# Router scores with the router weights stationary, an earlier load of the projection weights, and an expert-weight row copied from PSUM, in a transformer layer with eight experts

## The chip, the cores and the metric

The kernel runs on all 8 cores of one Trainium2 chip, each core doing one of the 8 batch elements with the same program. The metric is the device time of the slowest core in microseconds; lower is better.

## The reference

x is 8 x 2048 x 1024. The layer is attention, a residual and a layer norm, then a mixture of experts, a residual and a layer norm:

```python
x = _layernorm(x + _L0_attn_ref(x, W_attn, b_attn, W_proj, b_proj))
x = _layernorm(x + _L0_ffn_ref(x, router_w, ..., down_b))
...
scores = h @ router_w.T + router_b
vals, idx = jax.lax.top_k(scores, TOP_K)
vals = jax.nn.softmax(vals, axis=-1)
cw = jnp.sum(jax.nn.one_hot(idx, N_EXPERTS) * vals[..., None], axis=1)
for e in range(N_EXPERTS):
    g = h @ gate_up_w[e].T + gate_up_b[e]
    out = out + (_swiglu(g) @ down_w[e].T + down_b[e]) * cw[:, e:e + 1]
```

There are 16 heads of 64, rotary embedding, causal attention, 8 experts of hidden size 1024, and the two best experts of each token have weight. The kernel computes all 8 experts for all tokens; cw is zero for the others.

## The kernel before

Activations lie with features on the 128 partitions: 8 chunks of 128 features, 2048 tokens along the free axis, handled in 4 stretches (tt) of 512 tokens. A core goes through five stages one after the other.

1. QKV (L455, L476), bf16 matmuls with float32 sums in PSUM.
2. Attention, two heads at a time: scores (L647, L653), exponential on ScalarE (L664), mask on GpSimd (L672), sum with V (L686, L693). VectorE takes each result out of PSUM (ytst, L711) and SyncE stores it to ys_d in DRAM.
3. Projection and first layer norm, by tt. SyncE loads the softmax sums (srow) and then the attention result (ytsl) from ys_d, ScalarE's or SyncE's queue the residual (xfsl). The inverse sums are spread by a matmul with the selection matrix sel (pbc, L858), VectorE scales ytsl (L863), then 64 matmuls with wproj (pp, L878), residual, bias, and the layer norm in float32 in acc (`_ln_stats`, `_ln_apply`). `_ln_apply` spreads two rows of 512 float32 values with one-row matmuls (L252, L254). The result goes as bf16 to x1_d.
4. Router, in float32 from acc: scores (prt, L979), copied from PSUM to sctm (L987), top two and softmax on VectorE and ScalarE (L991 to L1029) into cwtm, 16 transposes (L1041), and a copy to cwT16 (L1045), which holds one expert's weights in each of 8 rows. cwrow0 is a zeroed tile of 128 partitions whose row 0 holds the current expert's row; a matmul with ones (pcw, L1228) spreads it.
5. Experts: for each e and tt, 8 times 8 gate matmuls (pg, L1283) and 8 up matmuls (pu, L1291), the activation, and the down matmuls of the stretch before (pd, L1136). Expert weights (wg in two halves, lo and hi; wd) are loaded ahead by SyncE and GpSimd. The last layer norm ends the program.

Each engine runs its instructions in the order in which they are written, and each DMA is issued from an engine's queue: channels dy0 to dy4 are SyncE's, dg0 to dg2 GpSimd's, dsc0 and dsc1 ScalarE's. Every channel has a semaphore. `E.dma` (L81) waits until the DMA issued last on its channel has landed. `E.w(consumer, tokens)` puts a wait into one engine's queue. `E.bar()` gives the present count of every engine's and every channel's semaphore, so `E.w("dy", *E.bar())` stops SyncE until all that has been issued so far in the program's text is done, DMAs included:

```python
    def bar(self):
        return tuple((k, self.cnt[k]) for k in self.cnt)
```

Such a wait for everything stands ahead of stage 3 on the queues of GpSimd, SyncE and ScalarE (dg, dy, dsc), because the tiles of that stage lie where attention's lay, and again ahead of stage 5.

Of the kernel before, what the change touches and what calls it, by code (L numbers as in the profile page):

```python
# [7 lines left out]
F32 = mybir.dt.float32  # L8
BF16 = mybir.dt.bfloat16
# [4 lines left out]
T = 2048  # L14
D = 1024
NCH = 8
NEXP = 8
# [258 lines left out]
def build_nc():  # L276
    nc = bass.Bass("TRN2", target_bir_lowering=False)
# [41 lines left out]
    with ExitStack() as st:  # L319
        a = st.enter_context  # L320
        E = Emit(nc, st)
        pe, act, dve = nc.tensor, nc.scalar, nc.vector
# [3 lines left out]
        rwt = a(nc.sbuf_tensor("rwt_s", [128, NCH * NEXP], F32))  # L326
# [11 lines left out]
        cwT16 = a(nc.sbuf_tensor("cwT16", [128, T], BF16))  # L338

        t_bqk = E.dma("dy4", bqk[:], bqk_i)  # L340
        t_bproj = E.dma("dy3", bproj[:], bproj_i)
        t_rwt = E.dma("dy2", rwt[:], rwt_i)
        t_rbr = E.dma("dy1", rbr_row[:], rbr_i)
        tok_zpad = E.tk(dve.memset(dbt16[:], 0.0), "dve")
        tok_zcw = E.tk(dve.memset(cwT16[:], 0.0), "dve")
        E.w("dg", tok_zpad)
# [8 lines left out]
        with nc.sbuf_tensor("gub_s", [128, NEXP * 16], F32) as gub, \  # L355
# [4 lines left out]
            for e2 in range(NEXP):  # L360
# [13 lines left out]
            tok_mm = E.tk(pe.matmul(pbi[:, 0:8], onesrf[0:1, :], rbr_row[0:1, :],  # L374
                                    start=True, stop=True), "pe")
# [4 lines left out]
        t_attn_done = None  # L380
        t_yt_dma = None
        with ExitStack() as s12:
# [25 lines left out]
            with ExitStack() as s1:  # L408
# [23 lines left out]
                with nc.psum_tensor("pq0", [128, 512], F32) as pq0, \  # L432
# [8 lines left out]
                    for tt in range(4):  # L441
                        par = tt % 2
# [298 lines left out]
        with ExitStack() as s3:  # L741
# [13 lines left out]
                    for i in range(2)]  # L755
# [11 lines left out]
            E.w("dg", *E.bar())  # L767
            E.w("dy", *E.bar())
            E.w("dsc", *E.bar())
            t_sel = E.dma("dg0", sel16[:], sel_i)  # L770
            rs_z = [E.tk(dve.memset(rs16[i][:], 0.0), "dve") for i in range(2)]
# [3 lines left out]
                           wproj_i[:, p * QWP:(p + 1) * QWP]) for p in range(4)]  # L775

# [193 lines left out]

            with nc.psum_tensor("prt2", [128, 128], F32) as prt2:
                E.mode(("mm", "k128", "f32"))
                mm_last = None
                for tt in range(4):
                    E.w("pe", t_rwt, tok_ln1_mul[tt])
                    for q_ in range(4):
                        ti = tt * 4 + q_
                        for c in range(NCH):
                            mm_last = pe.matmul(  # L979
                                prt2[:, ti * NEXP:(ti + 1) * NEXP],  # L980
                                acc[:, c * T + tt * 512 + q_ * 128:
                                    c * T + tt * 512 + (q_ + 1) * 128],
                                rwt[:, c * NEXP:(c + 1) * NEXP],
                                start=(c == 0), stop=(c == NCH - 1))
                tok_mm = E.tk(mm_last, "pe")
                E.w("dve", tok_mm)
                tok_sctm = E.tk(dve.tensor_copy(sctm[:], prt2[:, 0:128]), "dve")  # L987
                E.w("pe", tok_sctm)
# [47 lines left out]
            with nc.psum_tensor("prt3", [128, 2048], F32) as prt3:  # L1036
                E.mode(("tr", "f32"))
                E.w("pe", tok_cw, t_id)
                tr_tok = None
                for ti in range(16):  # L1040
                    tr = pe.transpose(prt3[0:NEXP, ti * 128:(ti + 1) * 128],  # L1041
                                      cwtm[:, ti * 8:(ti + 1) * 8], ident[:, 0:128])
                    tr_tok = E.tk(tr, "pe")
                E.w("dve", tr_tok)
                tok_cwT16 = E.tk(dve.tensor_copy(cwT16[0:NEXP, :],  # L1045
                                                 prt3[0:NEXP, 0:2048]), "dve")
                E.w("pe", tok_cwT16)

        dbias_ev = {}
        with ExitStack() as s5:  # L1050
# [9 lines left out]
            cwrow0 = b5(nc.sbuf_tensor("cwrow0", [128, T], BF16))  # L1060
# [33 lines left out]
            tok_crz = E.tk(dve.memset(cwrow0[:], 0.0), "dve")  # L1094
            E.w("dg", tok_cwT16, tok_crz)
            t_cwrow = [E.dma("dg0", cwrow[0][0:1, :], cwT16[0:1, :]), None]
# [307 lines left out]
```

How the kernel before makes its waits and increments, by code:

```python
    def tk(self, instr, key, step=1):  # L45
        self.cnt[key] += step
        instr.then_inc(self.sem[key], step)
        return (key, self.cnt[key])
# [1 line left out]
    def w(self, consumer, *tokens):  # L50
        eng = self.eng[consumer]
        best = {}
        for tok in tokens:
            if tok is None:
                continue
            key, val = tok
            if val > best.get(key, -1):
                best[key] = val
        for key, val in best.items():
            ck = (consumer, key)
            if self.wcache.get(ck, 0) >= val:
                continue
            eng.wait_ge(self.sem[key], val)
            self.wcache[ck] = val
# [9 lines left out]
    def dma(self, ch, out, in_):  # L74
        eng = self.dmaeng[ch]
        if self.cnt[ch]:
            ck = ("q" + ch, ch)
            if self.wcache.get(ck, 0) < self.cnt[ch]:
                eng.wait_ge(self.sem[ch], self.cnt[ch])
                self.wcache[ck] = self.cnt[ch]
        return self.tk(eng.dma_start(out=out, in_=in_), ch, 16)
```

## Time and profile before

| | |
|---|---|
| median of the runs shown | 2650.16 us (two runs: 2594.32 and 2706.0) |
| the profiled execution's own time | 2439.51 us |
| its span, slowest of the cores (core 3) | 2437.9 us |
| span of the fastest core (core 0) | 2424.8 us |
| mean granted TensorE clock, core 3 | 0.907 |

### The profile page before, as it was taken

The numbers are of one execution on the slowest core, as the hardware profiler recorded it, in microseconds if no ns is written. First come the engines' busy times: TensorE is split into PE (matmuls) and PEld (weight loads), VectorE is DVE, ScalarE is ACT, GpSimd is POOL, SyncE is SP. The second block draws the span as 40 slices with busy tenths as digits, with TensorE's granted clock in tenths as the row PEclk, the third lists the DMA queues.
The fourth block names the chain that finished last, engine by engine and source line by source line (L and its number), as shares of the span: only waits on it lengthen the run. The fifth ranks groups of instructions, "written<-read, shape, count | busy, mean of one in ns | idle before, by whom it ended". The sixth has DMA issues, their size and how long they took to land.

```text
span 2437.9 us, 26649 instructions; the slowest of 8 cores (2424.8 to 2437.9 us)
## 1 busy us (share of the span) xinstructions
PE 2062.6 (85%) x8982; PEld 912.7 (37%) x8982; DVE 933.4 (38%) x1982; ACT 942.0 (39%) x1336; POOL 162.0 (7%) x248
## 2 busy tenths in 40 slices
PE   6996776777745766999999999999999999999974
PEld 2442222222212254443443443443444444444431
DVE  3106323232025431444444444444444443444456
ACT  2233666666624520432332332332333333333541
POOL 1000222111110100000000000000000000000100
PEclk9997888888867855999999999999999999999986
DMA  6300111111054023110301301301302113011002
GB/s 147 52 13 14 33 28 27 27 27 27 10 145 121 18 70 121 69 35 20 128 26 35 121 18 35 122 18 35 121 18 92 64 35 121 18 35 52 18 31 108
DMA packets 39978, 137.67 MB, mean 56 GB/s; under 512 B 5852, under 2 KB 19549, under 8 KB 30886
## 3 DMA queue, kind: packets, MB, share of 16 engines
q1 hardware_dynamic: 27412, 83.95, 10.7%
q0 software_dynamic: 9888, 47.30, 6.2%
q10 hardware_dynamic: 2546, 4.72, 0.6%
q8 instruction: 75, 1.23, 0.2%
q14 instruction: 57, 0.47, 0.1%
HBM read 116.28 MB, written 16.84 MB: 55 GB/s over the span
## 4 chain that ended last, share of the span: by engine, by line
PE 74%; ACT 8%; DVE 7%; DMA 4%; issue 4%; POOL 2%; DVEq 0%; ACTq 0%; SPq 0%; POOLq 0%
PE pg L1283 18%; PE pu L1291 18%; PE pd L1136 18%; ACT attAB L664 6%; PE pq L455 3%; PE pp L878 3%; PE psy L686 3%; PE pv L476 2%; PE prt L979 2%; POOL attAB L672 2%; DVE acc L264 2%; DVE acc L261 2%; PE psab L653 2%; PE psy L693 2%; PE psab L647 2%
## 5 line engine op out<-in xcount | busy, mean ns | idle before, releaser
L1304 ACT ACTIVATE sgt<-pg,gubs_s 128x512 bf16<-128x512 f32 x256 | 176.3, 689 | 920.0 <-PE pu L1291 887.3
L1283 PE MATMUL pg<-x1sl,wg 128*128 128x512 bf16 x2048 | 492.3, 384 | 4.1 <-DMA wg<-wg 4.1
L1136 PE MATMUL pd<-as,wd 128*128 128x512 bf16 x2048 | 484.9, 380 | 12.7 <-DVE acc L1146 12.1
L1291 PE MATMUL pu<-x1sl,wg 128*128 128x512 bf16 x2048 | 484.8, 380 | 0.0
L664 ACT ACTIVATE attAB<-psab,consts_s 128x1024 bf16<-128x1024 f32 (+1 forms) x320 | 302.7, 985 | 189.1 <-PE psab L653 188.2
L1319 DVE TENSOR_SCALAR gct<-gct 128x512 bf16<-128x512 bf16 x256 | 75.2, 294 | 748.6 <-ACT uct L1312 748.6
L1283 PEld LDWEIGHTS pg<-x1sl,wg 128*128 128x128 bf16 x2048 | 202.3, 99 | 252.7 <-issue 17.4
L1136 PEld LDWEIGHTS pd<-as,wd 128*128 128x128 bf16 x2048 | 200.6, 98 | 257.0 <-issue 17.3
L1291 PEld LDWEIGHTS pu<-x1sl,wg 128*128 128x128 bf16 x2048 | 200.8, 98 | 243.0 <-issue 2.4
L686 PE MATMUL psy<-attAB,vaug 128*65 128x512 bf16 (+1 forms) x320 | 124.2, 388 | 142.4 <-POOL attAB L672 88.2
L1146 DVE TENSOR_TENSOR acc<-acc,pd 128x512 f32<-128x512 f32 x256 | 174.1, 680 | 8.8 <-PE pd L1136 8.8
L1312 ACT ACTIVATE uct<-pu,gub_s 128x512 bf16<-128x512 f32 x256 | 176.9, 691 | 0.0
L1308 ACT ACTIVATE gct<-pg,gub_s 128x512 bf16<-128x512 f32 x256 | 174.6, 682 | 0.0
L711 DVE CAST ytst<-psy 65x1024 bf16<-65x1024 f32 x32 | 38.9, 1218 | 259.0 <-PE psy L693 209.6
L686 PEld LDWEIGHTS psy<-attAB,vaug 128*65 128x65 bf16 x320 | 37.4, 117 | 268.6 <-issue 267.7
L647 PE MATMUL psab<-qkraw 128*128 128x512 bf16 (+1 forms) x320 | 127.9, 400 | 7.6 <-DVE qkraw L597 7.6
L653 PE MATMUL psab<-qkraw,kpadB 128*128 128x512 bf16 (+1 forms) x320 | 126.9, 397 | 0.0
L693 PE MATMUL psy<-attAB,vaug 128*65 128x512 bf16 (+1 forms) x320 | 125.1, 391 | 0.0
L672 POOL TENSOR_TENSOR attAB<-attAB,cmask_s 128x256 bf16<-128x256 bf16 x128 | 93.5, 739 | 467.8 <-ACT attAB L664 465.5
L455 PE MATMUL pq<-xsl,wqk 128*128 128x512 bf16 x512 | 112.6, 382 | 11.2 <-DMA wqk<-wqk 11.2
L1337 DVE TENSOR_TENSOR as<-gct,uct 128x512 bf16<-128x512 bf16 x256 | 108.8, 425 | 28.4 <-DVE uct L1329 2.3
L1326 DVE TENSOR_TENSOR gct<-gct,sgt 128x512 bf16<-128x512 bf16 x256 | 107.5, 420 | 1.5 <-DVE uct L1322 1.5
(154 smaller groups left out, 1344.1 us busy)
## 6 DMA issues: line engine op xcount, KB each, us to landing
x1sl<-x_d SPq DMA_DIRECT2D x30, 1024.0 KB
wg<-wg SPq DMA_DIRECT2D x8, 2048.0 KB
wg<-wg POOLq DMA_DIRECT2D x8, 2048.0 KB, 17.0
wd<-wd POOLq DMA_DIRECT2D x14, 1024.0 KB, 5.5
out<-acc SPq DMA_DIRECT2D x29, 256.0 KB, 2.3
qswp<-qkraw SPq DMA_DIRECT2D x56, 128.0 KB
ys_d<-ytst SPq DMA_DIRECT2D x64, 65.0 KB
xsl<-x_t POOLq DMA_DIRECT2D x4, 1024.0 KB, 11.2
```

The lines of the kernel that those rows point to most:

```text
L455: mm_last = pe.matmul(pq[mp][:, 0:512], wqk16[:, (m * NCH + c) * 128:(m * NCH + c + 1) * 128], xsl[par][:, c * 512:(c + 1) * 512], start=( ...
L647: mA = pe.matmul(psAB[par][:, 0:w_], qkraw[:, kcol + 128 * j:kcol + 128 * j + 128], qkraw[:, qcol + tqs:qcol + tq0 + 512], start=True, sto ...
L653: mB = pe.matmul(psAB[par][:, 512:512 + w_], kpadB[:, cch * T + 128 * j:cch * T + 128 * j + 128], qkraw[:, qcol + tqs:qcol + tq0 + 512], s ...
L664: eAB = act.activation(dst3, src3, AF.Exp, bias=consts[:, 0:1], scale=0.125)
L686: aA = pe.matmul(psy[qp][0:65, tqs - tq0:512], vaug[:, j * 1056 + hA * 66: j * 1056 + hA * 66 + 65], attAB[ab][:, 0:w_], start=(j == 0), s ...
L1136: mmd = pe.matmul(pd[dp][:, 0:512], wdb[:, (m2_ * NCH + hc_) * 128:(m2_ * NCH + hc_ + 1) * 128], asb[tp_][:, hc_ * 512:(hc_ + 1) * 512], s ...
L1146: tok = E.tk(dve.tensor_tensor(acc[:, sl], acc[:, sl], pd[dp][:, 0:512], ALU.add), "dve")
L1283: mmg = pe.matmul(pg[hp][:, 0:512], wgb[ep][:, (hc * NCH + c) * 128:(hc * NCH + c + 1) * 128], x1sl[k % 2][:, c * 512:(c + 1) * 512], star ...
L1291: mmu = pe.matmul(pu[hp][:, 0:512], wgb[ep][:, ((hc + 8) * NCH + c) * 128: ((hc + 8) * NCH + c + 1) * 128], x1sl[k % 2][:, c * 512:(c + 1) ...
L1304: tok_sg = E.tk(act.activation(sg_t[hp][:], pg[hp][:], AF.Sigmoid, bias=gubs[:, bg:bg + 1], scale=1.702), "act")
L1308: tok_rg = E.tk(act.activation(gc_t[hp][:], pg[hp][:], AF.Relu, bias=gub7[:, bg:bg + 1], scale=1.0), "act")
L1312: tok_ru = E.tk(act.activation(uc_t[hp][:], pu[hp][:], AF.Relu, bias=gub7[:, bu:bu + 1], scale=1.0), "act")
```

## The change

There are three edits.

The router's scores are computed the other way round. Before, a slice of acc of 128 features by 128 tokens was stationary and the 8 columns of router weights moved past it (128 matmuls of the program). Now the 128 x 8 router weights are stationary and 512 tokens of acc move (32 matmuls). The result lies as 8 rows by 512 tokens, so VectorE copies it to sct after each stretch, and 16 transposes bring it into the shape that the following code expects.

```diff
+            with nc.psum_tensor("prt0", [128, 512], F32) as prt0, \
+                 nc.psum_tensor("prt1", [128, 512], F32) as prt1:
+                E.mode(("mm", "k128m8", "f32"))
+                sc_ev = []
+                for tt in range(4):
+                    par = tt % 2
+                    if tt >= 2:
+                        E.w("pe", sc_ev[tt - 2])
+                    E.w("pe", t_rwt, tok_ln1_mul[tt])
+                    mm_last = None
+                    for c in range(NCH):
+                        mm_last = pe.matmul(
+                            [prt0, prt1][par][0:NEXP, 0:512],
+                            rwt[:, c * NEXP:(c + 1) * NEXP],
+                            acc[:, c * T + tt * 512:c * T + (tt + 1) * 512],
+                            start=(c == 0), stop=(c == NCH - 1))
+                    tok_mm = E.tk(mm_last, "pe")
+                    E.w("dve", tok_mm)
+                    iv = dve.tensor_copy(sct[:, tt * 512:(tt + 1) * 512],
+                                         [prt0, prt1][par][0:NEXP, 0:512])
+                    sc_ev.append(E.tk(iv, "dve"))
...
-                        for c in range(NCH):
-                            mm_last = pe.matmul(
-                                prt2[:, ti * NEXP:(ti + 1) * NEXP],
-                                acc[:, c * T + tt * 512 + q_ * 128:
-                                    c * T + tt * 512 + (q_ + 1) * 128],
-                                rwt[:, c * NEXP:(c + 1) * NEXP],
-                                start=(c == 0), stop=(c == NCH - 1))
...
+                E.w("pe", t_id, *sc_ev)
+                for ti in range(16):
+                    tr = pe.transpose(prt2[:, ti * 8:(ti + 1) * 8],
+                                      sct[:, ti * 128:(ti + 1) * 128],
+                                      ident[0:8, 0:8])
```

On TensorE this is, from the end of the last layer norm to the transposes of the gate weights (prt is the scores' PSUM tile, acc the activations, rwt_s the router weights, sct the scores by rows, cwtm the gate weights), before:

```order
L252 MATMUL plb<-srB,onesrf_s 128x512 [waits sem_act,sem_dve]
L254 MATMUL plb<-srC,onesrf_s 128x512
L979 MATMUL prt<-rwt_s,acc 128x8 [waits sem_act]
L979 MATMUL prt<-rwt_s,acc 128x8 x95
L979 MATMUL prt<-rwt_s,acc 128x8 [waits sem_dve]
L979 MATMUL prt<-rwt_s,acc 128x8 x31
L1041 MATMUL prt<-ident_s,cwtm 8x128 [waits sem_dve,sem_dy4]
L1041 MATMUL prt<-ident_s,cwtm 8x128 x15
```

and now:

```order
L254 MATMUL plb<-srC,onesrf_s 128x512
L986 MATMUL prt<-acc,rwt_s 8x512 [waits sem_act]
L986 MATMUL prt<-acc,rwt_s 8x512 x15
L986 MATMUL prt<-acc,rwt_s 8x512 [waits sem_dve]
L986 MATMUL prt<-acc,rwt_s 8x512 x7
L986 MATMUL prt<-acc,rwt_s 8x512 [waits sem_dve]
L986 MATMUL prt<-acc,rwt_s 8x512 x7
L1003 MATMUL prt<-ident_s,sct 128x8 [waits sem_dve,sem_dy4]
L1003 MATMUL prt<-ident_s,sct 128x8 x15
L1062 MATMUL prt<-ident_s,cwtm 8x128 [waits sem_dve]
```

The 128 matmuls have become 32 and 16 transposes, and both runs of matmuls start on the same wait, for ScalarE's last cast of the layer norm.

Ahead of stage 3 the loads of sel and of the four quarters of wproj are issued before the wait for everything, when the last attention result is out of PSUM (t_attn_done). The wait itself now stands behind them:

```diff
-            E.w("dg", *E.bar())
-            E.w("dy", *E.bar())
-            E.w("dsc", *E.bar())
+            E.w("dg", t_attn_done)
+            E.w("dy", t_attn_done)
             t_sel = E.dma("dg0", sel16[:], sel_i)
-            rs_z = [E.tk(dve.memset(rs16[i][:], 0.0), "dve") for i in range(2)]
             QWP = 2 * NCH * 128
             t_wp4 = [E.dma(("dg0", "dg1", "dg2", "dy4")[p],
                            wproj16[:, p * QWP:(p + 1) * QWP],
                            wproj_i[:, p * QWP:(p + 1) * QWP]) for p in range(4)]
+            E.w("dg", *E.bar())
+            E.w("dy", *E.bar())
+            E.w("dsc", *E.bar())
+            rs_z = [E.tk(dve.memset(rs16[i][:], 0.0), "dve") for i in range(2)]
```

On SyncE's queue, from the last stores of attention to the first loads of the projection stage (- is before, + is now):

```order
 L81 DMA ys_d<-ytst 65x512 [waits sem_dve,sem_dy3]
 L81 DMA ys_d<-ytst 65x512 [waits sem_dy3]
-L81 DMA wproj<-wproj 128x2048 [waits sem_pe,sem_act,sem_pool,sem_dy0,sem_dy1,sem_dy2,sem_dy3,sem_dy4,sem_dg0,sem_dg1,sem_dg2,sem_dsc0,sem_dsc1]
-L81 DMA srow_0<-ys_d 8x512 [waits sem_dy0] x2
+L81 DMA wproj<-wproj 128x2048 [waits sem_dy4]
+L81 DMA srow_0<-ys_d 8x512 [waits sem_pe,sem_act,sem_pool,sem_dy0,sem_dy1,sem_dy2,sem_dy3,sem_dy4,sem_dg0,sem_dg1,sem_dg2,sem_dsc0,sem_dsc1]
+L81 DMA srow_0<-ys_d 8x512 [waits sem_dy0]
 L81 DMA ytsl<-ys_d 64x4096 [waits sem_dy0]
 L81 DMA ytsl<-ys_d 64x4096 [waits sem_dy1]
```

The long wait has moved from ahead of wproj to ahead of srow, and its counts of dg0, dg1, dg2 and dy4 now include the loads just issued.

Ahead of stage 5, row 0 of cwrow0 for the first expert is copied by VectorE straight from PSUM. cwrow0 is allocated and zeroed at the program's start; before, it was zeroed here and filled by a DMA on GpSimd's queue:

```diff
+                tok_cwr0 = E.tk(dve.tensor_copy(cwrow0[0:1, :],
+                                                prt3[0:1, 0:2048]), "dve")
...
-            tok_crz = E.tk(dve.memset(cwrow0[:], 0.0), "dve")
-            E.w("dg", tok_cwT16, tok_crz)
-            t_cwrow = [E.dma("dg0", cwrow[0][0:1, :], cwT16[0:1, :]), None]
+            E.w("dg", tok_cwT16)
+            t_cwrow = [tok_cwr0, None]
```

## Rows read from the trace of the kernel before

**Rows 1.** The page, part 2: granted TensorE clock in 40 slices, tenths

```profile
PEclk9997888888867855999999999999999999999986
```

**Rows 2.** The page, part 4: shares of the chain of waits, by line

```profile
PE pg L1283 18%; PE pu L1291 18%; PE pd L1136 18%; ACT attAB L664 6%; PE pq L455 3%; PE pp L878 3%; PE psy L686 3%; PE pv L476 2%; PE prt L979 2%; POOL attAB L672 2%; DVE acc L264 2%; DVE acc L261 2%; PE psab L653 2%; PE psy L693 2%; PE psab L647 2%
```

**Rows 3.** Groups of instructions: the router's matmuls and its weight loads; stationary size precedes moving

```profile
L979 PE MATMUL prt<-rwt_s,acc 128*128 128x8 f32 x256 | 54.8, 361 | 12.3 <-ACT x1b L270 12.3
L979 PEld LDWEIGHTS prt<-rwt_s,acc 128*128 128x128 f32 x256 | 54.7, 333 | 13.9 <-issue 13.9
```

**Rows 4.** Windows: us, busy (count) by engine, TensorE clock share, DMA share, GB/s

```profile
714.00:719.00 5.00, 4.85 (x12) 1.80 (x13) 0.69 (x2) 0.26 (x1) 0.00 (x0) 0.50 0.95 207
...
884.60:939.50 54.90, 54.78 (x256) 54.69 (x256) 0.00 (x0) 0.00 (x0) 0.00 (x0) 0.50 0.17 59
945.00:949.00 4.00, 3.22 (x16) 1.83 (x16) 0.42 (x2) 0.00 (x0) 0.00 (x0) 0.62 0.00 0
```

**Rows 5.** Chain of waits, float32 512-column matmuls: start us, us, what

```profile
851.63 0.87 PE plb L254 x2
...
870.62 1.72 PE plb L254 x2
```

**Rows 6.** Groups of instructions: float32 weight load of eight columns

```profile
L1041 PEld LDWEIGHTS prt<-ident_s,cwtm 128*8 128x8 f32 x16 | 1.8, 118 | 7.0 <-issue 5.9
```

**Rows 7.** Timeline, end of the layer norm and router: start us, us, engine, line

```profile
863.72 0.67 DVE L221 TENSOR_SCALAR srC<-pstat 1x512 f32<-1x512 f32 x1
...
884.66 54.78 PE L979 MATMUL prt<-rwt_s,acc 128*128 128x8 f32 x256 [12.34 <-ACT x1b L270]
...
939.55 0.29 DVE L987 COPY sctm<-prt 128x128 f32<-128x128 f32 x1 [55.92 <-PE prt L979]
```

**Rows 8.** Timeline, from gate weights to the load of wg

```profile
945.28 3.22 PE L1041 MATMUL prt<-ident_s,cwtm 128*8 128x128 f32 x16 [5.83 <-DVE cwtm L1029]
948.61 2.28 DVE L1045 CAST cwT<-prt 8x2048 bf16<-8x2048 f32 x1 [3.58 <-PE prt L1041]
951.26 1.76 DVE L1094 MEMSET cwrow<- 128x2048 bf16 x1 [0.38 <-issue]
951.57 0.33 SPq L81 DMA_DIRECT2D wg<-wg  x1
953.67 0.51 POOL L81 DMA_DIRECT2D cwrow<-cwT  x1 [101.07 <-DVE cwrow L1094]
954.18 0.55 POOL L81 DMA_DIRECT2D wg<-wg  x1
```

**Rows 9.** Timeline, first matmuls of the experts

```profile
967.80 3.57 PE L1283 MATMUL pg<-x1sl,wg 128*128 128x512 bf16 x8 [4.10 <-DMA wg<-wg]
```

**Rows 10.** Timeline, attention's end to the projection's start

```profile
677.96 1.99 SPq L81 DMA_DIRECT2D ys_d<-ytst  x2
681.68 0.36 SPq L81 DMA_DIRECT2D wproj<-wproj  x1
...
682.23 0.62 POOL L81 DMA_DIRECT2D sel<-sel  x1 [6.41 <-DMA ys_d<-ytst]
```

**Rows 11.** Chain of waits, same place

```profile
682.15 8.05 DMA srow<-ys_d
...
690.26 5.11 DMA srow<-ys_d
...
696.02 12.03 DMA ytsl<-ys_d
```

**Rows 12.** DMA issues: KB each, median us from issue to landing

```profile
wd<-wd POOLq DMA_DIRECT2D x14, 1024.0 KB, 5.5
...
wproj<-wproj POOLq DMA_DIRECT2D x3, 512.0 KB, 7.8
...
cc<-cc POOLq DMA_DIRECT2D x1, 512.0 KB, 5.8
...
sel<-sel POOLq DMA_DIRECT2D x1, 256.0 KB, 10.1
```

More of the change, by code:

```diff
@@ L338, in build_nc @@
         cwT16 = a(nc.sbuf_tensor("cwT16", [128, T], BF16))
+        cwrow0 = a(nc.sbuf_tensor("cwrow0", [128, T], BF16))
         t_bqk = E.dma("dy4", bqk[:], bqk_i)
@@ L345, in build_nc @@
         tok_zcw = E.tk(dve.memset(cwT16[:], 0.0), "dve")
+        tok_crz = E.tk(dve.memset(cwrow0[:], 0.0), "dve")
         E.w("dg", tok_zpad)
@@ L969, in r3 @@
                 return ap.rearrange("p (t e) -> p t e", e=NEXP)
-            with nc.psum_tensor("prt2", [128, 128], F32) as prt2:
[L972 to L977, printed above, removed]
-                        for c in range(NCH):
-                            mm_last = pe.matmul(
-                                prt2[:, ti * NEXP:(ti + 1) * NEXP],
-                                acc[:, c * T + tt * 512 + q_ * 128:
-                                    c * T + tt * 512 + (q_ + 1) * 128],
-                                rwt[:, c * NEXP:(c + 1) * NEXP],
-                                start=(c == 0), stop=(c == NCH - 1))
-                tok_mm = E.tk(mm_last, "pe")
-                E.w("dve", tok_mm)
+            with nc.psum_tensor("prt0", [128, 512], F32) as prt0, \
[19 more added lines that the diff above has]
+                    sc_ev.append(E.tk(iv, "dve"))
+                E.w("pe", *sc_ev)
@@ L987, in build_nc @@
+            with nc.psum_tensor("prt2", [128, 128], F32) as prt2:
+                E.mode(("tr", "f32"))
+                E.w("pe", t_id, *sc_ev)
+                tr_tok = None
+                for ti in range(16):
+                    tr = pe.transpose(prt2[:, ti * 8:(ti + 1) * 8],
+                                      sct[:, ti * 128:(ti + 1) * 128],
+                                      ident[0:8, 0:8])
+                    tr_tok = E.tk(tr, "pe")
+                E.w("dve", tr_tok)
                 tok_sctm = E.tk(dve.tensor_copy(sctm[:], prt2[:, 0:128]), "dve")
@@ L1037, in build_nc @@
                 E.mode(("tr", "f32"))
-                E.w("pe", tok_cw, t_id)
+                E.w("pe", tok_cw)
                 tr_tok = None
@@ L1043, in build_nc @@
                     tr_tok = E.tk(tr, "pe")
-                E.w("dve", tr_tok)
+                E.w("dve", tr_tok, tok_crz)
                 tok_cwT16 = E.tk(dve.tensor_copy(cwT16[0:NEXP, :],
                                                  prt3[0:NEXP, 0:2048]), "dve")
+                tok_cwr0 = E.tk(dve.tensor_copy(cwrow0[0:1, :],
+                                                prt3[0:1, 0:2048]), "dve")
                 E.w("pe", tok_cwT16)
@@ L1059, in build_nc @@
             cwb = b5(nc.sbuf_tensor("cwb16", [128, T], BF16))
-            cwrow0 = b5(nc.sbuf_tensor("cwrow0", [128, T], BF16))
             cwrow = [cwrow0, cwrow0]
```

## The prediction

> **What bounds the kernel now.** I read the spans of the cores first, then the chain of waits by line, then the clock row, then the stages that the change touches in windows and as a timeline. The chain says where a saved microsecond counts: gate, up and down matmuls hold 18% each, and the router's L979 holds 2% [rows 2], so nothing here can touch the bulk. But the router is a stretch where TensorE alone decides: its two records for each of 128 matmuls are busy 54.8 us, its weight loads 54.7 us [rows 3], nothing else runs, and VectorE waits 55.92 us for the end [rows 7]. The reader should see that the weight loads are as long as the matmuls: 54.78 / 256 = 0.214 us a record, for 8 moving columns. The clock row has its two lowest slices there [rows 1], and the window shows 0.50, 1.2 GHz, through all 54.9 us although the engine never paused [rows 4]. The other touched place is the hand-over from attention to the projection, where the chain runs through DMAs: srow 8.05, srow 5.11, ytsl 12.03 us [rows 11].
>
> **The router matmuls.** They leave with 54.78 us. In their place stand 32 matmuls of 512 moving float32 columns, two records each, so 64. The nearest rows are the one-row float32 matmuls of the layer norm, also 512 columns in two records: 0.87 us for the pair at high clock, 1.72 us at 1.2 GHz [rows 5]. So 64 records take 32 x 0.87 = 27.8 us, or 32 x 1.72 = 55.0 us at the low clock. Which one? The engine comes in at the low clock, after 12.34 us idle [rows 7]. After such an idle time the projection's bf16 matmuls of 512 columns ran at 0.50 for 5 us [rows 4] and the first 3.57 us of the experts were slow as well [rows 9]; then both went high. The L979 stream stayed low, but even the 16 transposes of 128 moving columns behind it, 3.22 us of work, sit in a window whose mean is 0.62 [rows 4, 8]. The two streams that rose were 512-column matmuls like the new ones, so I take their course, 3.5 to 5 us at half speed, which costs half of that, 2.2 us. The matmuls end 30.0 us after the same start, 884.66, at 914.7.
>
> Behind them is new work. VectorE's four PSUM copies of 8 x 512 overlap the matmuls but for the last: 0.67 us by a one-row op of that width [rows 7], and 0.2 us to start. Then TensorE restarts (0.25 us) and does 16 transposes. Their stationary side is 128 float32 columns, like the L979 loads at 0.214 us a record at the low clock; each transpose is one record (16 for 16 in rows 8), so 3.4 us at most and 1.7 us if the clock is high just behind the stream. I take 2.1 with the latency of the last, and 0.3 to the copy of sctm. Sum 884.66 + 30.0 + 0.2 + 0.67 + 0.25 + 2.1 + 0.3 = 918.2, against 939.55 [rows 7]: 21.3 us earlier. All that follows up to the experts hangs on this, one engine after the other, so it arrives whole. The identity matrix is loaded on SyncE's queue as before and is first needed some 30 us into the router rather than 60; nothing ahead of it is new.
>
> The eight-column weight loads are the open cost. One takes 118 ns [rows 6], and I count them at nothing because the load of the next record hides behind the 435 ns of the present one, as 128-column loads do inside the 0.87 us pair. The Trainium skill, "TensorE: Matmul & The Clock Gate", Part 3, says that a weight load overlaps a matmul in flight only when its row group differs, and here all use all 128 rows. By that rule 64 x 118 ns = 7.6 us would be added and the gain would be 13.7 us. The row of the pair speaks against it, though its weights have one row; I keep this as a rival.
>
> **The row for the first expert.** Before, from the start of the cwT16 copy at 948.61: copy 2.28, memset of cwrow to 953.02, cwrow's DMA at 953.67, wg lo at 954.18 on GpSimd; SyncE issues wg hi at 951.57 [rows 8]. Now the memset is at the program's start (1.76 us on VectorE, under the first loads) and a copy of 1 x 2048 follows. Its length is not in the trace; VectorE's time goes by the free size (0.67 us for one row of 512 above), so I take the 2.28 us of the 8-row copy. The count that both queues wait for now includes this copy: 948.61 + 2.28 + 0.1 + 2.28 = 953.27. GpSimd, 0.65 us later as before, issues wg lo at 953.9, 0.3 us earlier; SyncE, 0.68 us behind as before, issues wg hi at 953.95, 2.4 us later. The gate matmuls wait for lo (967.80, [rows 9]), and hi is wanted only one group of 8 matmuls later, 3.57 us. With hi's head start gone, lo gets no less of the DMA engines. I take -0.3 us, between -1 and +2. Queued behind on GpSimd is wd, not wanted before the second stretch.
>
> **The earlier load.** This is the part with two sides. The loads of sel and of the SyncE quarter of wproj go out some 4 and 1.7 us earlier, at about 678.1 and 680.0 instead of 682.23 and 681.68 [rows 10]. But the three waits for everything now stand behind them, and everything includes their own semaphores. SyncE may not issue srow, and ScalarE not xfsl, before all of wproj has landed. GpSimd still waits for sel before its first quarter (10.1 us, [rows 12]), with the other two behind it in the queue. Nobody else is queued there that matters: GpSimd's next work is a cast after the first projection matmuls.
> So, step by step: sel is half of cc, which took 5.8 us; alone I take 4.5, landing at 683.2. The three quarters, 1.5 MB, go out by 684.8 and land in 6.5 us or so (7.8 beside ytsl in rows 12, 1 MB of wd in 5.5): 691.5. SyncE then issues srow at 691.9 instead of 682.15, 9.8 us late. What comes back is contention: the first srow took 8.05 us beside sel, xfsl and a quarter of wproj; now only xfsl is beside it, as beside the second, 5.11 us. ytsl took 12.03 us beside 1.5 MB of wproj, now alone 5.6 us by the 1 MB wd row. Arrival: 691.9 + 5.1 + 5.1 + 0.9 + 5.6 = 708.6, against 696.02 + 12.03 = 708.05 [rows 11]. That is +0.5 us: the same bytes in another order, an earlier start against two more stops. From below: if the srow pair takes 2 x 2 us, -6. From above: sel 10.1 again, wproj 9, srow 8.05 and 5.11, ytsl 6, about +15.
>
> The srow step rests on order within a queue. By the Trainium skill, "DMA: Bandwidth & Descriptors", Queues, rings and completion order, each DMA engine takes turns between queue rows and works in order within one. Then the first srow stood behind SyncE's own quarter of wproj, and would not now, so it may fall below 5 us. Rows 11 only show that the first was slower than the second.
>
> **Sum.** -21.3 - 0.3 + 0.5 = -21.1 us of the profiled execution's 2439.5: 2418.4. The two timed runs have their median at 2650.2, 1.086 times the profiled time, and lie 4.3% apart. On that scale the same share of the time is 21.1 x 1.086 = 22.9 us, and 2650.2 - 22.9 gives 2627. I state this one, since it is to be held against runs like those shown, and the range must know both levels. The change is -0.9%; about 2% is what a measurement of this kernel can tell from no change.
>
> **Rivals.**
> 1. Slower: the clock stays at 1.2 GHz through the new router matmuls. For it: L979, back to back for 55 us, did not lift it [rows 4], and both streams are float32 with the same operands. Against: bf16 streams of that width rose, and the float32 pair kept 0.435 us a record behind one [rows 5]. Price: 55.0 + 0.2 + 0.67 + 0.25 + 3.4 + 0.3 = 59.8 us from 884.66, ending 944.5, 4.9 us late: 2444.6, or 2655.5 on the scale of the runs. It decides from a mean record of about 0.77 us, where the new stream with its tail equals the old. Chance 0.12.
> 2. The wait behind its own loads costs its upper bound, because sel needs 10 us even alone: +15, total -6: 2433.7 (2644). Chance 0.14. For it: GpSimd's casting load was the slowest of its size. Against: cc casts too, twice as large, in 5.8.
> 3. Weight loads are not hidden: -13.5, 2426.0 (2635.5). Chance 0.07.
> 4. The earlier load pays, -6 there: -27.6, 2411.9 (2620). Chance 0.09.
> 5. My forecast, a gain of 17 to 26 us: 0.58, its own range 2413 to 2423 on the profiled execution, 2622 to 2632 on the scale of the runs.
>
> All five lie within 2%, so 0.80 for no change that can be told. The rest is the scatter of runs 4.3% apart, leaning to the forecast's sign: faster 0.14, slower 0.06. The range is not set by the terms but by the level: it reaches from the profiled level with the full gain, 2411, to the higher run shown less the gain, 2706 - 23 = 2683.
>
> **What would show it.** Right: 64 router records of about 0.43 us with the clock at 1.0 after some 4 us; sctm's copy some 34 us after the last cast of the layer norm; wg hi issued beside lo; srow issued near 692 with all of wproj landed, and ytsl's first scaling near 708.6. Wrong: records near 0.85 us, weight loads standing between matmuls, the first pp matmul later than 716 or earlier than 710, or the experts' up matmuls waiting for wg hi.

## The result and the profile after

| | before | changed |
|---|---|---|
| median of all timed runs | 2463.5 us (10 runs, 2438.7 to 2759.0) | 2421.1 us (11 runs, 2418.3 to 2752.0) |
| ratio | | 0.9917, 95% interval 0.9904 to 0.9930 |
| profiled execution, its own time | 2439.5 us | 2418.7 us |
| span of the slowest core | 2437.9 us (core 3) | 2417.1 us (core 4) |
| mean granted clock of that core | 0.907 | 0.914 |

The change gains 0.83%, 20.2 us of 2440; the profiled executions are 20.8 us apart. Four of the eleven runs of the changed kernel (2510.8 to 2752.0 us) had the four cores of one die at 0.79 to 0.88 of full clock while the other die stayed near 0.915, and the ratio leaves such runs out.

The page of the changed kernel, the clock in 40 slices and the shares of the chain, which answer to [rows 1] and [rows 2]:

```profile
PEclk9997888888867777999999999999999999999986
...
PE pg L1304 19%; PE pu L1312 18%; PE pd L1157 18%; ACT attAB L666 6%; PE pq L457 5%; PE psy L688 3%; PE pp L882 3%; POOL attAB L674 2%; PE pv L478 2%; DVE acc L264 2%; PE psab L655 2%; PE psab L649 2%; DVE acc L261 2%; PE psy L695 2%; PE prt L986 1%
```

The two slices that were 5 are now 7, and the router's line has fallen from 2% to 1% of the chain. Gate, up and down stand as they did, within 1% of the span.

One core is not enough to place a microsecond: in the kernel before, the hand-over from attention takes 27.7 to 31.5 us on the eight cores. So the stages were read from the timelines of all eight, as the time between two starts, and the table gives the median over the cores.

| from start to start, us | before | changed | difference | forecast |
|---|---|---|---|---|
| last copy of attention's result (ytst) to first scaling of ytsl | 29.21 | 30.19 | +1.0 | +0.5 |
| to the first pp matmul | 6.01 | 6.01 | 0 | 0 |
| to the first router matmul | 169.53 | 169.60 | +0.1 | 0 |
| to the copy of sctm | 54.89 | 32.66 | -22.2 | -21.3 |
| to the copy of cwT16 | 9.12 | 9.30 | +0.2 | 0 |
| to the first expert matmul | 17.85 | 19.65 | +1.8 | -0.3 |
| to the end | 1469.70 | 1470.08 | +0.4 | 0 |

These add up to -18.7; the medians of stages need not add to the difference of two slowest cores.

The router first. Groups of instructions of the changed kernel, answering to [rows 3]:

```profile
L986 PE MATMUL prt<-acc,rwt_s 128*8 128x512 f32 x64 | 30.4, 640 | 12.3 <-ACT x1b L270 12.3
...
L986 PEld LDWEIGHTS prt<-acc,rwt_s 128*8 128x8 f32 x64 | 6.0, 94 | 37.4 <-issue 37.4
...
L1003 PE MATMUL prt<-ident_s,sct 8*128 8x8 f32 x16 | 1.1, 201 | 1.1 <-DVE sct L993 1.1
```

64 records stand in place of 256. The 64 weight loads are busy 6.0 us, but the matmuls take 30.4 us, against 27.8 us of streaming at the high clock and 2.2 us more for the slow start, so next to nothing of the 6.0 stands between them. The windows of the same stretch (us, then busy time and count of PE, PEld, DVE, ACT, POOL, then granted clock, DMA share, GB/s) show the slow start, which answers to [rows 4]:

```profile
883.70:888.00 4.30, 4.30 (x6) 0.72 (x7) 0.00 (x0) 0.00 (x0) 0.00 (x0) 0.50 0.71 244
888.00:890.00 2.00, 2.00 (x5) 0.38 (x4) 0.00 (x0) 0.00 (x0) 0.00 (x0) 0.67 0.00 0
890.00:900.00 10.00, 10.00 (x25) 2.07 (x23) 0.68 (x1) 0.00 (x0) 0.00 (x0) 1.00 0.64 217
900.00:913.00 13.00, 13.00 (x31) 2.70 (x30) 1.36 (x2) 0.00 (x0) 0.00 (x0) 1.00 0.01 1
```

For 4.3 us the clock is 0.50 and the window touches six records, in the next two it rises, and from 890 on the windows touch 25 in 10 us. The timeline of VectorE behind it, answering to [rows 7], has the last copy to sct and the copy of sctm:

```profile
914.20 0.68 DVE L993 COPY sct<-prt 8x512 f32<-8x512 f32 x1 [6.19 <-PE prt L986]
916.44 0.29 DVE L1008 COPY sctm<-prt 128x128 f32<-128x128 f32 x1 [1.55 <-PE prt L1003]
```

2.24 us lie between their starts. I had put 3.3; the 16 transposes take 1.1 us in all and not 2.1.

Then the start of the experts, answering to [rows 8] and [rows 9]:

```profile
925.75 2.28 DVE L1066 CAST cwT<-prt 8x2048 bf16<-8x2048 f32 x1 [3.82 <-PE prt L1062]
927.95 2.27 DVE L1068 CAST cwrow<-prt 1x2048 bf16<-1x2048 f32 x1
...
930.76 0.33 SPq L81 DMA_DIRECT2D wg<-wg  x1
931.33 0.53 POOL L81 DMA_DIRECT2D wg<-wg  x1 [79.54 <-issue]
...
946.97 3.57 PE L1304 MATMUL pg<-x1sl,wg 128*128 128x512 bf16 x8 [13.09 <-DMA wg<-wg]
```

The row copy takes 2.27 us, as forecast. Both halves of wg are now issued within 0.6 us of each other, and lo, 15.1 us after its issue has ended, is what the first gate matmul waits for; before, it was 13.1 us. The pcw matmuls, which spread the row and waited for cwrow's DMA before, are done long ahead and gain nothing.

The chain through the hand-over (start us, us, what), answering to [rows 11]:

```profile
679.04 4.01 DMA sel<-sel
...
684.67 7.81 DMA wproj<-wproj
...
692.69 2.82 DMA srow<-ys_d
...
695.59 4.70 DMA srow<-ys_d
...
700.94 6.76 DMA ytsl<-ys_d
```

sel takes 4.0 us instead of 10.1. All of wproj is down at 692.5, and only then may srow go; but srow is now 2.8 and 4.7 us instead of 8.1 and 5.1, ytsl 6.8 instead of 12.0. Over the eight cores the first srow took 4.7 to 8.0 us before and takes 1.4 to 3.1 now, ytsl 10.3 to 13.2 before and 6.5 to 7.8 now.

### The profile page after: what moved, and what is told of

The parts are those of the page before. It is cut to its first block, busy times and chain, and to the rows that moved or that the text cites. A ratio compares the mean times of both kernels' runs of the same rounds, so it can differ in the third digit from the quotient of the medians.

```text
span 2417.1 us, 26296 instructions; the slowest of 8 cores (2407.1 to 2417.1 us)
## 1 busy us (share of the span) xinstructions
PE 2042.8 (85%) x8806; PEld 866.4 (36%) x8806; DVE 938.2 (39%) x1987; ACT 939.6 (39%) x1336; POOL 160.8 (7%) x247
## 4 chain that ended last, share of the span: by engine, by line
PE 75%; ACT 8%; DVE 7%; issue 4%; DMA 3%; POOL 2%; DVEq 0%; ACTq 0%; POOLq 0%; SPq 0%
PE pg L1304 19%; PE pu L1312 18%; PE pd L1157 18%; ACT attAB L666 6%; PE pq L457 5%; PE psy L688 3%; PE pp L882 3%; POOL attAB L674 2%; PE pv L478 2%; DVE acc L264 2%; PE psab L655 2%; PE psab L649 2%; DVE acc L261 2%; PE psy L695 2%; PE prt L986 1%
## 5 line engine op out<-in xcount | busy, mean ns | idle before, releaser
L1304 PE MATMUL pg<-x1sl,wg 128*128 128x512 bf16 x2048 | 492.1, 384 | 13.1 <-DMA wg<-wg 13.1
L457 PE MATMUL pq<-xsl,wqk 128*128 128x512 bf16 x512 | 112.6, 382 | 10.2 <-DMA wqk<-wqk 9.3
```

The source lines that it names most:

```text
L457: mm_last = pe.matmul(pq[mp][:, 0:512], wqk16[:, (m * NCH + c) * 128:(m * NCH + c + 1) * 128], xsl[par][:, c * 512:(c + 1) * 512], start=( ...
L1304: mmg = pe.matmul(pg[hp][:, 0:512], wgb[ep][:, (hc * NCH + c) * 128:(hc * NCH + c + 1) * 128], x1sl[k % 2][:, c * 512:(c + 1) * 512], star ...
```

## The experiments

Eleven kernels were run. The first four take the change apart. Each ratio is to the kernel before, run on the same chip.

**router_only.** The kernel before with the router edit and nothing else.

> The kernel before with the router edit alone. Theory (each edit acts in its own stage and the stages are in series): the router, from its first matmul to the copy of sctm, shrinks from 54.9 to 32.8 us as in the changed kernel, the two other stages stay as before, and the time falls by 22 us (ratio 0.991). Rival (part of the gain comes from the other edits, or the experts' start takes some back because wg is then late): a gain of 18 us or less.

Measured: 2420.0 us, ratio 0.9920 (0.9902 to 0.9938). First router matmul to sctm 32.6 us, cwT16 to the first expert matmul 17.85 as before, hand-over 29.4. The theory holds: the router edit alone gives the whole gain. What the two other edits cost in the table, 2.8 us, is too little for the two kernels' times to show (2420.0 and 2421.1 us).

**load_only.** The kernel before with only the earlier load.

> The kernel before with the earlier load of sel and wproj alone. Theory (the same bytes in another order): from the last copy of the attention result to the first pp matmul 36.6 us instead of 37.5, so -0.9 us (ratio 0.9996). Rival (the difference of 0.9 us between the two profiles is scatter of the DMAs): anything between -3 and +3 us, and another split over sel, wproj, srow and ytsl than 4.0, 7.8, 2.8 + 4.7 and 6.8 us.

Measured: 2441.3 us, ratio 1.0002 (0.9991 to 1.0012). Over the hand-over its eight cores took 29.6 to 31.8 us, though in an execution of 2562.8 us. The other kernels settle it: in the four without the earlier load (before, router_only, cwrow_only, old_router_warmed) the eight-core medians are 29.0 to 29.4 us, in the six with it and with the wait behind it (the changed kernel, row_not_waited, wd_after_lo, router_128, router_in_the_gap, wg_early) 30.0 to 30.6. The gain of 0.9 us that I read from two slowest cores was the scatter of one core: the theory's sign is wrong, and the eight-core table, +1.0 us, is right. The split on core 3 is as in the changed kernel (sel 4.4, wproj 6.9, srow 3.0 and 4.6, ytsl 6.7).

**cwrow_only.** The kernel before with only the row copied from PSUM.

> The kernel before with the row for the first expert copied from PSUM alone. Theory (wg hi loses its head start of 2.6 us, all three weight loads start together and wg lo lands later): from the start of the cwT16 copy to the first expert matmul 21.2 us instead of 19.2, +2.0 us in all (ratio 1.0008). Rival (the 2 us belong to the earlier time at which the load falls in the changed kernel, or to scatter): 19.2 us as before, +-0.3 us.

Measured: 2443.2 us, ratio 1.0012 (1.0002 to 1.0023). cwT16 to the first expert matmul: median 20.2 us against 17.85, so +2.35. This edit takes away a DMA and a memset and still costs time, and its interval lies above 1.

**wait_old_counts.** The changed kernel, with the wait taken from older counts:

```diff
+            bar0 = E.bar()
             E.w("dg", t_attn_done)
             E.w("dy", t_attn_done)
...
-            E.w("dg", *E.bar())
-            E.w("dy", *E.bar())
-            E.w("dsc", *E.bar())
+            E.w("dg", *bar0)
+            E.w("dy", *bar0)
+            E.w("dsc", *bar0)
```

> The changed kernel, with the wait for everything ahead of the projection stage taken from counts read before the loads of sel and wproj are issued, so it waits for attention only. Theory (the same bytes with fewer stops): srow is issued near 682 again, the two gaps of the DMA engines (685 to 687 and 691 to 695) close, ytsl lands 3 to 6 us earlier than in the changed kernel: -4 us, ratio to before 0.990. Rival (contention comes back and eats the head start): srow again 8 and 5 us, ytsl 12 us, the first pp matmul where it is now within 1.5 us, ratio 0.992.

Measured: 2418.0 us, ratio 0.9909 (0.9893 to 0.9924); hand-over 29.4 us, 0.8 less than in the changed kernel and as before. The chain of the core that ended last:

```profile
682.75 1.62 DMA ys_d<-ytst
...
684.43 4.12 DMA ys_d<-ytst
...
688.97 2.89 DMA srow<-ys_d
...
691.93 5.20 DMA srow<-ys_d
...
697.78 9.39 DMA ytsl<-ys_d
```

The last store of ys_d takes 4.1 us beside sel instead of 1.6 (2.6 to 4.1 over the eight cores, 1.6 on all of them before), so srow goes out 7.6 us after the start of the last ytst copy, not 5.5 as before; the second srow and ytsl take 5.2 and 9.4 us beside wproj. But this core is not typical: its hand-over takes 25.9 us, the shortest of the eight. On six of the eight cores the chain goes another way, through xfsl, the residual that ScalarE's queue loads; core 5, first its chain, then its timeline:

```profile
683.57 22.58 DMA xfsl<-x_t
...
706.28 1.01 PE L863 MATMUL pbc<-rs,sel 128*128 128x512 bf16 x2 [30.47 <-DMA xfsl<-x_t]
```

xfsl, in flight beside wproj, srow and ytsl, takes 21.4 to 22.6 us on these six cores. The first pbc matmul waits for it although it reads only rs and sel: the program has this wait (t_xfs) ahead of the pbc matmuls, in the kernel before too. So the rival was the better picture in its price, contention that eats the head start, but not in its place. The wait for its own loads costs about 1 us, not 4. What the hand-over would take with the wait for xfsl moved to where it is needed wasn't run.

**row_not_waited.** The changed kernel; the wait ahead of the experts leaves out the row copy:

```diff
+                bar_row = E.bar()
                 tok_cwr0 = E.tk(dve.tensor_copy(cwrow0[0:1, :],
...
-            E.w("dg", *E.bar())
-            E.w("dsc", *E.bar())
-            E.w("dy", *E.bar())
+            E.w("dg", *bar_row)
+            E.w("dsc", *bar_row)
+            E.w("dy", *bar_row)
```

> The changed kernel, with the wait of SyncE's and GpSimd's queues ahead of the experts taken from counts read before the row copy, so both halves of wg go out when cwT16 is written. Theory (lo shares the DMA engines with hi from its issue on, whatever the start): both are issued some 2.3 us earlier, lo still takes about 15.1 us, and from the start of the cwT16 copy to the first expert matmul the mean falls from 19.65 to 17.4 us: -2.3 us against the changed kernel. Rival (the row copy itself, or the pcw matmuls, become the wait): 19 us or more.

Measured: 2419.8 us, ratio 0.9898 (0.9842 to 0.9954, too wide to tell 2 us). The stage is plain: median 17.38 us against 19.65, forecast 17.4. The timeline of its slowest core (start us, us, engine, line):

```profile
923.42 2.28 DVE L1066 CAST cwT<-prt 8x2048 bf16<-8x2048 f32 x1 [3.82 <-PE prt L1062]
925.63 2.27 DVE L1069 CAST cwrow<-prt 1x2048 bf16<-1x2048 f32 x1
926.18 0.33 SPq L81 DMA_DIRECT2D wg<-wg  x1
926.80 0.53 POOL L81 DMA_DIRECT2D wg<-wg  x1 [77.40 <-issue]
...
942.39 3.57 PE L1305 MATMUL pg<-x1sl,wg 128*128 128x512 bf16 x8 [10.85 <-DMA wg<-wg]
```

hi leaves while the row copy has only begun, lo 0.6 us behind it, and lo again takes 15.1 us from the end of its issue. So the 2 us are lo's longer flight and not the length of the row copy. All eight cores say on what the flight depends. In the three kernels where hi is issued 2.6 us ahead of lo (before, router_only, old_router_warmed) lo's flight has a mean of 11.5 to 11.7 us, in the seven where it is 0.6 us ahead 13.3 to 13.9. Counted from the end of hi's issue to the first gate matmul, though, the mean is 14.1 to 14.7 us in all ten: hi's issue sets the stage. Here lo is issued 2.2 us earlier than in the kernel before, and the stage's mean is only 0.4 us shorter than there.

**wd_after_lo.** The changed kernel; wd waits for lo:

```diff
+            E.w("dg", t_wg[0][0])
             _t0 = E.dma("dg2", wdb[:], wd_i[0])
```

> The changed kernel, with the first wd load issued only when wg lo has landed. Theory (wd takes a share of the DMA engines from lo): 4 MB instead of 6 are in flight ahead of the first expert matmul, lo takes 12.5 to 13.5 us instead of 15.3, -2 us. Rival (lo and wd are on one queue, GpSimd's, and are worked off in order, so wd takes nothing from lo; hi on SyncE's queue does): no change within 0.5 us, and wd later without anybody waiting for it.

Measured: ratio 0.9905 (0.9871 to 0.9940), stage 19.4 us against 19.65.

```profile
924.55 2.28 DVE L1066 CAST cwT<-prt 8x2048 bf16<-8x2048 f32 x1 [3.82 <-PE prt L1062]
...
929.56 0.33 SPq L81 DMA_DIRECT2D wg<-wg  x1
930.14 0.53 POOL L81 DMA_DIRECT2D wg<-wg  x1 [79.16 <-issue]
...
944.42 3.57 PE L1305 MATMUL pg<-x1sl,wg 128*128 128x512 bf16 x8 [11.75 <-DMA wg<-wg]
944.68 0.53 POOL L81 DMA_DIRECT2D wd<-wd  x1 [14.02 <-DMA wg<-wg]
```

wd goes out at 944.7, when lo is down. lo takes 13.8 us on this core; over the eight cores the stage has a mean of 19.4 us (18.2 to 20.9) against 19.6 (17.6 to 21.3) in the changed kernel, so the cores lie closer together but gain next to nothing. The Trainium skill, "DMA: Bandwidth & Descriptors", Queues, rings and completion order, says that each DMA engine works in order within a queue row and takes turns between rows; lo and wd are both issued by GpSimd, hi by SyncE. This run agrees: wd took nothing from lo that can be seen. That leaves hi, whose lost head start is the 2 us; a kernel that copies the row and gives hi its head start back wasn't run.

**old_router_warmed.** The kernel before, with 44 matmuls in TensorE's idle time ahead of the old router. They add nothing to any result.

```diff
+                E.mode(("mm", "k128", "bf16"))
+                E.w("pe", ev_tok[6], ev_tok[7])
+                for _ in range(44):
+                    pe.matmul(ppr[0][:, 0:512], wproj16[:, 0:128],
+                              ytsl[1][:, 0:512], start=True, stop=True)
                 E.w("pe", tok_ln1[3])
```

> The kernel before, with 44 extra bf16 matmuls of 512 columns (their result is not used) in TensorE's idle time ahead of the router, so the old router starts at the high clock. Theory (the old stream itself does not hold the clock): the granted clock falls back to 0.50 within some us, the 256 records take 50 us or more, gain below 5 us. Rival (only the start counts, and the clock once high stays): all records at about 107 ns, 27.4 us, sctm copied 27 us earlier, so that the whole gain of the new form could be had without it.

Measured: ratio 0.9994 (0.9970 to 1.0018). Windows of the slowest core, where the old router starts at 885.1, and its group:

```profile
878.00:884.00 6.00, 5.95 (x28) 2.74 (x28) 5.58 (x9) 2.89 (x4) 0.00 (x0) 1.00 0.00 0
884.00:888.00 4.00, 3.32 (x24) 2.89 (x22) 0.08 (x1) 0.72 (x1) 0.00 (x0) 0.87 0.51 174
888.00:892.00 4.00, 4.00 (x21) 4.00 (x20) 0.00 (x0) 0.00 (x0) 0.00 (x0) 0.50 0.27 93
...
900.00:910.00 10.00, 10.00 (x49) 10.00 (x48) 0.00 (x0) 0.00 (x0) 0.00 (x0) 0.50 0.12 47
```

```profile
L984 PE MATMUL prt<-rwt_s,acc 128*128 128x8 f32 x256 | 53.1, 354 | 0.7 <-ACT x1b L270 0.7
```

The clock is 1.00 when the old stream starts and 0.50 from 888 on, with TensorE busy 100% of every window from there. The router takes 53.2 us instead of 54.9: a high clock at its start does not help the old form.

**router_128.** The changed kernel with narrower moving slices, 128 matmuls of the program:

```diff
-                    for c in range(NCH):
-                        mm_last = pe.matmul(
-                            [prt0, prt1][par][0:NEXP, 0:512],
-                            rwt[:, c * NEXP:(c + 1) * NEXP],
-                            acc[:, c * T + tt * 512:c * T + (tt + 1) * 512],
-                            start=(c == 0), stop=(c == NCH - 1))
+                    for q_ in range(4):
+                        for c in range(NCH):
+                            mm_last = pe.matmul(
+                                [prt0, prt1][par][0:NEXP, q_ * 128:(q_ + 1) * 128],
+                                rwt[:, c * NEXP:(c + 1) * NEXP],
+                                acc[:, c * T + tt * 512 + q_ * 128:
+                                    c * T + tt * 512 + (q_ + 1) * 128],
+                                start=(c == 0), stop=(c == NCH - 1))
```

> The changed kernel with the same stationary router weights but 128 instead of 512 moving tokens: 128 matmuls, 256 records. Theory (the swap of the sides is what counts: eight-column weight loads of 94 ns hide behind a record of 107 ns, and the stream reaches the high clock as the 512-column one does): the router takes 33 to 38 us. Rival (the narrower stream does not reach or hold 2.4 GHz, or the weight loads stand between the records): 50 us or more, as in the kernel before.

Measured: the profiled execution took 2418.7 us (four timed runs, 2417.8 to 2705.4, scattered too widely for a ratio); router to sctm 33.2 us against 32.7. Its groups:

```profile
L987 PE MATMUL prt<-acc,rwt_s 128*8 128x128 f32 x256 | 30.8, 288 | 12.3 <-ACT x1b L270 12.3
...
L987 PEld LDWEIGHTS prt<-acc,rwt_s 128*8 128x8 f32 x256 | 24.2, 95 | 20.3 <-issue 13.9
```

As many matmuls as in the kernel before and nearly the time of the new form. The weight loads, 24.2 us busy, still lie under the matmuls. What counts is which operand stands still, not the number of matmuls. The swap changes two things at once, 8 stationary columns for 128 and 128 moving ones for 8; which of them the clock answers to isn't separated.

**router_in_the_gap.** The changed kernel; the sums go to banks that the projection has done with, stretch 0 ahead of the last layer norm's spreading matmuls, 1 to 3 behind:

```diff
+                router_mm(0, pp0)
                 tok_n, pm_ = _ln_apply(nc, E, acc, x1b16, srBs[3], srCs[3],
...
+                router_mm(1, pp1)
+                router_mm(2, pbc0)
+                router_mm(3, pbc1)
+                s3p.close()
+                sct = b3(nc.sbuf_tensor("sct", [NEXP, T], F32))
+                sc_ev = []
+                for tt, bank in enumerate((pp0, pp1, pbc0, pbc1)):
+                    E.w("dve", sc_mm[tt])
+                    sc_ev.append(E.tk(dve.tensor_copy(
+                        sct[:, tt * 512:(tt + 1) * 512],
+                        bank[0:NEXP, 0:512]), "dve"))
```

> The changed kernel, with the router matmuls of the first stretch between the last layer norm statistics and its spreading matmuls, those of stretches 1 and 2 behind these, under VectorE's multiplications, and only stretch 3 after the last wait; four PSUM banks of the projection hold the sums and the four copies follow the layer norm on VectorE. Theory (TensorE idles 10.7 and 12.3 us there, and stretch 3 needs 6.9 us): the copy of sctm comes 20 to 22 us earlier, ratio to before 0.983. Rival (the three float32 stretches delay the spreading matmuls and the copies delay the layer norm, and the clock falls in between): a gain of 12 us or less, the spreading matmuls later than 868.6.

Measured: ratio 0.9850 (0.9774 to 0.9926), a wide interval from three runs of 2398.4, 2401.6 and 2411.7 us. The stage is plain: from the first pp matmul to sctm 181.4 us against 202.1 in the changed kernel and 224.4 before: -20.7 us, as the theory has it. TensorE in its slowest core:

```profile
852.87 7.03 PE L937 MATMUL pp<-acc,rwt_s 128*8 128x512 f32 x16
...
864.72 1.93 PE L252 MATMUL plb<-srB,onesrf_s 1*128 1x512 f32 x2 [4.82 <-DVE srC L237]
...
868.46 8.60 PE L937 MATMUL pp<-acc,rwt_s 128*8 128x512 f32 x16
...
876.90 13.90 PE L937 MATMUL pbc<-acc,rwt_s 128*8 128x512 f32 x32
...
893.13 0.29 DVE L1010 COPY sctm<-prt 128x128 f32<-128x128 f32 x1 [1.55 <-PE prt L1005]
```

Stretch 0 lies in the first gap, 1 and 2 run while VectorE multiplies, and the spreading matmuls start at 864.72, 0.15 us after VectorE has written the row that they need, as they did before. The copy of sctm waits for stretch 3 alone.

**wg_early.** The changed kernel; wg's and wd's first loads wait only for counts read at the end of the projection, and their tiles are allocated behind the small ones, where only projection tiles lay:

```diff
+                pre_wg = E.bar()
                 tok_n, pm_ = _ln_apply(nc, E, acc, x1b16, srBs[3], srCs[3],
...
+                pre_wg += (("pe", E.cnt["pe"]),)
...
+            E.w("dg", *pre_wg)
+            E.w("dy", *pre_wg)
             def load_wg(e, war=None):
...
+            E.w("dg", *bar_row)
+            E.w("dsc", *bar_row)
+            E.w("dy", *bar_row)
```

> The changed kernel, with the first loads of wg and wd issued when the projection's tiles are free (behind the last spreading matmuls) instead of behind the router; their tiles are placed where only projection tiles lay. Theory (the experts start late only because 6 MB are asked for after the gate weights are known): wg is there before it is wanted, the first expert matmul follows the pcw matmuls some 8 us after the start of the cwT16 copy instead of 19.65, -11.5 us, ratio to before 0.987. Rival (the loads collide with the stores and reloads of x1, or float32 matmuls slow down beside them): a gain of 8 us or less, or the router longer than 32.8 us.

Measured: 2409.4 us, ratio 0.9865 (0.9849 to 0.9880). The stage is 8.55 us on every core instead of 17.6 to 21.3, and the router keeps its 32.7 us beside the loads.

```profile
876.98 0.53 POOL L81 DMA_DIRECT2D wg<-wg  x1 [20.95 <-DVE acc L261]
...
902.39 0.33 SPq L81 DMA_DIRECT2D wg<-wg  x1
...
930.11 2.28 DVE L1068 CAST cwT<-prt 8x2048 bf16<-8x2048 f32 x1 [3.83 <-PE prt L1064]
...
938.66 3.24 PE L1310 MATMUL pg<-x1sl,wg 128*128 128x512 bf16 x8 [0.43 <-issue]
```

lo is issued at 877 and hi at 902, both while the router runs; the first gate matmul comes 8.55 us after the cwT16 copy, behind the pcw matmuls.

**combined.** wait_old_counts, router_in_the_gap and wg_early together.

> The changed kernel with the wait of the projection stage by the old counts, the router matmuls in TensorE's gaps, and the early loads of wg and wd. Theory (three separate stages, their gains add up: 0.8, 21 and 11.5 us): 2388 us, ratio to before 0.978. Rival (with the router short, wg hi on SyncE's queue, behind the stores and reloads of x1, lands after the first gate group): 2392 us or more, with the up matmuls waiting for wg.

Measured: 2385.0 us, ratio 0.9775 (0.9761 to 0.9789): 2.25% faster than the kernel before, and the best version here. The parts add up and a little more: 2421.1 less 0.8, 20.7 and 11.1 would be 2388.5 us. Of the rest, 1.2 us are in the hand-over, 28.2 us here; why isn't shown. The chain of its slowest core shows what is late next there:

```profile
882.30 6.86 DMA x_d<-x1b
889.23 3.66 DMA ident_s<-ident
...
893.17 1.14 PE prt L1008 x16
```

The load of the identity matrix, issued by SyncE behind the stores of x1, is the last thing that the transposes wait for on this core; on four of the eight cores the chain goes through these stores and this load, on the other four through TensorE's matmuls. hi was not a wait; the rival did not come.

## Why the prediction was right or wrong

**The router matmuls: right.** Forecast 30.0 us for the 64 records; 30.4 us measured. The course of the clock was as taken from rows of before (4.3 us at 0.50, then up), and the fear behind rival 1 did not come. The steps had the number but not what it says: at the low clock the new form would take 55.0 us, as long as the old one. So the whole gain is the clock. What keeps the clock down is the old stream itself (old_router_warmed), and the swap of the operands ends it (router_128).

**The weight loads: right.** Counted at nothing, and they cost nothing: one starts every 0.43 us and lasts 0.09. The rule of the Trainium skill in "TensorE: Matmul & The Clock Gate", Part 3, by which a load overlaps a matmul only in another row group, would have added 6.0 us, an estimate with the measured loads; the measurement decides against it, here and in router_128, where 24.2 us of loads hide under 30.8 of matmuls.

**The tail of the router: mis-sized by 1 us.** 2.1 us for the transposes and their latency, 1.1 measured.

**The earlier load: right in kind, +0.5 forecast, +1.0 measured.** sel 4.5 forecast and 4.0 measured, the quarters down at 691.5 forecast and 692.5 measured, ytsl 5.6 forecast and 6.8 measured. The srow pair took 7.5 us on the core shown, not 10.2. Of the first srow I had said that it might fall below 5 us once it no longer stood behind SyncE's own quarter of wproj: it took 2.8; whether its own queue or the emptier DMA engines did it, no run separates. Waiting for its own loads, the trap in this edit, costs 1 us only (wait_old_counts).

**The row for the first expert: the step failed.** It said "With hi's head start gone, lo gets no less of the DMA engines. I take -0.3 us". lo takes 2 us more (13.5 against 11.6, the means of eight cores), since hi had moved bytes in its 2.6 us alone and now competes with lo for them. lo's issue didn't come the forecast 0.3 us earlier either: it starts 5.58 us after the cwT16 copy, 5.57 before. Measured +1.8 us in the change and +2.35 alone; inside the bounds of -1 to +2 for the first, outside for the second. The cause was tested from both sides: issue both earlier and lo's flight stays the same (row_not_waited); hold back wd and next to nothing changes (wd_after_lo).

**The sum: right on one scale, wrong on the one stated.** -21.1 us of 2439.5 gave 2418.4 us for an execution like the profiled one; 2418.7 came. That it fits to 0.3 us is luck: by the eight-core stages the change is -18.7 us, the router 0.9 us better than forecast and the two load stages together 2.6 us worse. But the step "On that scale the same share of the time is 21.1 x 1.086 = 22.9 us, and 2650.2 - 22.9 gives 2627. I state this one" took two runs for the kernel's level that lay 6 and 11% above the others. With more runs the kernel before has five of its ten at 2438.7 to 2442.5, and the changed one its median at 2421.1: the stated 2627 is 206 us off, none of it from a term of the sum. This is the step that failed. The profile had said so: eight cores within 13 us of each other at one clock, and 2439.5 us; two runs 112 us apart could not both be the kernel's time, and the profiled execution, with the same clock on all its cores, was the one to go by. The statement that about 2% can be told was too coarse as well: the interval is 0.26% wide, and the gain of 0.83% stands clear of it.

**The rivals.** None of the four came: the clock rose, sel took 4.0 us alone, the weight loads were hidden, and the earlier load did not pay. By its own terms the second one's total is -6.6 us and its time 2432.9, not 2433.7. No change beyond 2% had 0.80, and the ratio lies within it.

## What to carry to other kernels

Where one side of a small matmul is 8 wide, let that side stand still: TensorE then streams columns instead of loading weights, and in this case that alone brought the clock from 1.2 to 2.4 GHz and the stage from 55 to 33 us. A wait for everything issued so far is a snapshot: read it before the loads that should run ahead of it, and where a load is moved, ask which other load on another queue had a head start. More than the change gave lay in the idle engines that it left, each found as a gap in the timeline: TensorE under the layer norm (20.7 us) and the DMA engines under the router (11.1 us). And look at which operation carries a wait: here the first pbc matmul waited for a residual that it doesn't read.

## What was not expected of the hardware

The old router kept TensorE busy in every window, and the granted clock fell from 1.00 to 0.50 within about 3 us of its start (885.1 to 888 in the windows of old_router_warmed). A busy engine can run at the low clock for 50 us.

The last small store of ys_d, 65 KB, went from 1.6 us on every core to between 2.6 and 4.1 when a load was put beside it (wait_old_counts), and everything behind the wait moved with it.

Eight cores running the same program do not wait equally long for the same loads: in the changed kernel wg lo made the stage 17.6 us on some cores and 21.3 on others. Why these cores and not those stays open; it wasn't tried.
